# The last feed-forward chunk's way out, spread over the first head of the second attention

## The reference

```
# feed-forward (D_HID = 512)
h = silu(x @ w1.T * w1_s) * (x @ w2.T * w2_s)
h = gelu(h @ h1.T * h1_s)
h = gelu(h @ h2.T * h2_s)
y = h @ w3.T * w3_s                        # 512 -> 128: "the way out"

# differential attention, 8 heads, two components of 8 per head
L1, L2 = cosine scores of component 1 and 2, scaled per head
G  = tanh(delta_gain * (L1 - L2))
A1 = softmax(L1 + G);  A2 = softmax(L2 - G)
y  = (A1 - lambda * A2) @ v,  an RMS norm per head, then @ Wo.T + bo
```

## Time and profile before

| | us |
|---|---|
| median of 3 runs | 706.14 |
| lowest, highest | 706.1, 706.49 |
| the profiled execution | 707.33 |
| its span | 705.5 |
| PE busy | 635.1 (90%) |
| DVE busy | 534.8 (76%) |
| ACT busy | 481.2 (68%) |
| POOL busy | 184.4 (26%) |

### The profile page before, as it was taken

How to read it: one execution, slowest core, us unless ns; L and a number is a source line. 1 busy time by engine, 2 the same in 40 slices (tenths; PEclk the granted TensorE clock), 3 DMA queues, 4 the chain that set the end, 5 groups by cost and what they waited for, 6 DMA issues and landing times.

```text
span 705.5 us, 9380 instructions
## 1 busy us (share of the span) xinstructions
PE 635.1 (90%) x3320; PEld 271.9 (39%) x3320; DVE 534.8 (76%) x1011; ACT 481.2 (68%) x479; POOL 184.4 (26%) x238
## 2 busy tenths in 40 slices
PE   8988899999999989889988888898898788899996
PEld 4666445464464523223222211122231111266555
DVE  6988421517246289999999999999999999676775
ACT  3545324234334399999999999999999989544431
POOL 3431060212102031491147200805600006022012
PEclk9999999999999999999999999999999989999999
DMA  6700200001304402234022510121011204300171
GB/s 193 234 21 1 91 1 0 1 1 36 99 0 135 113 1 57 57 87 140 21 57 84 163 47 11 57 57 56 23 35 57 57 2 121 119 1 1 38 233 30
DMA packets 33598, 44.74 MB, mean 63 GB/s; under 512 B 5520, under 2 KB 19728, under 8 KB 33168
## 3 DMA queue, kind: packets, MB, share of 16 engines
q1 hardware_dynamic: 33552, 44.15, 21.5%
HBM read 31.47 MB, written 10.55 MB: 60 GB/s over the span
## 4 chain that ended last, share of the span: by engine, by line
PE 40%; DVE 23%; ACT 23%; issue 11%; DMA 1%; POOL 1%; SPq 0%; DVEq 0%; ACTq 0%
ACT w_hh L1045 19%; PE ps L731 8%; PE ps L741 8%; DVE hid L1377 5%; DVE hid L1372 5%; PE ps L766 5%; PE ps L713 4%; PE ps L643 3%; PE ps L624 3%; PE ps L697 2%; PE ps L775 2%; DVE st L1147 2%; ACT probs L1016 2%; DMA x_res<-in_x 1%; DVE mx L1224 1%
## 5 line engine op out<-in xcount | busy, mean ns | idle before, releaser
L1045 ACT ACTIVATE w_hh<-hid 128x2048 f32<-128x2048 f32 x128 | 249.9, 1952 | 8.4 <-DVE hid L1377 7.9
L643 PE MATMUL ps<-w_hh,v_h 128*32 128x512 f32 x1024 | 137.8, 610 | 33.3 <-ACT w_hh L1045 32.0
L1372 DVE TENSOR_TENSOR hid<-ps,probs 128x1024 f32<-128x1024 f32 x86 | 104.7, 1217 | 19.3 <-ACT probs L1016 16.1
L624 PE MATMUL ps<-q_s,k_s 64*128 64x512 bf16 x256 | 99.4, 389 | 14.8 <-DVE hid L1372 14.2
L1377 DVE SCALAR_TENSOR_TENSOR hid<-ps,probs 128x1024 f32<-128x1024 f32 x86 | 104.8, 1219 | 4.4 <-PE ps L624 3.3
L624 PE MATMUL ps<-q_w,k_w 64*128 64x512 bf16 x256 | 99.4, 389 | 0.0
L1016 ACT ACTIVATE probs<-ps 128x1024 f32<-128x1024 f32 x86 | 91.2, 1061 | 2.3 <-PE ps L624 2.3
L624 PE MATMUL ps<-q_g,k_s 128*128 128x512 bf16 x256 | 78.3, 388 | 1.1 <-ACT qkv_a L1016 1.1
L624 PEld LDWEIGHTS ps<-q_w,k_w 64*128 64x128 bf16 x256 | 23.7, 93 | 107.2 <-issue 54.5
L741 PE MATMUL ps<-hid,w_hh 128*128 128x512 f32 x128 | 56.3, 592 | 0.0
L731 PE MATMUL ps<-hid,w_hh 128*128 128x512 f32 x128 | 55.8, 593 | 0.0
(11 more groups left out here) (298 smaller groups left out, 991.2 us busy)
## 6 DMA issues: line engine op xcount, KB each, us to landing
qk_rows<-part SPq DMA_DIRECT2D x48, 128.0 KB, 2.4
w_hh<-w_rows SPq DMA_DIRECT2D x4, 1024.0 KB, 9.6
qk_rows<-part_g SPq DMA_DIRECT2D x24, 128.0 KB, 2.4
q_g<-qk_rows SPq DMA_DIRECT2D x32, 96.0 KB, 2.2
k_s<-qk_rows SPq DMA_DIRECT2D x32, 96.0 KB, 2.2
q_s<-qk_rows SPq DMA_DIRECT2D x32, 96.0 KB, 2.4
k_w<-qk_rows SPq DMA_DIRECT2D x32, 96.0 KB, 2.5
q_w<-qk_rows SPq DMA_DIRECT2D x32, 96.0 KB, 2.4
```

The source lines that it names most:

```text
L624: last = mm(ps[:, base + half, :], k_op[rows, u, keys], q_op[rows, u, half * CHUNK:(half + 1) * CHUNK], start=True, stop=True)
L643: last = mm(ps[VW * g4:VW * g4 + VW, 6, :], v_h[:, u, mt, :], ee[:, mt % 2, g4 * CHUNK:(g4 + 1) * CHUNK], start=(mt == 0), stop=(mt == BT ...
L1045: A(ee[:, mt % 2, :], zz[:, mt % 2, :], ACT.Exp).then_inc(S["e"], 1)
L1372: v.tensor_tensor(zz[:, mt % 2, 0:SEQ], banks[:, 2 * CHUNK:4 * CHUNK], gg[s % 3], ALU.add).then_inc(S["z1"], 1)
```

## The change

The table of turns is moved: those of chunk 2 four steps later (v 0 five), those of chunk 3 two to four steps later (late turn one, sums 1 one). The four tiles of the last feed-forward chunk go into the turn bank, one each in the steps (0,1), (0,3), (0,5), (0,7), behind `c_first` and ahead of `c_values`. `b_evac` moves from (0,1) to (1,0), still between the two sums, `b_stats` from (0,2) to (1,1), and the statistics of chunk 3 (`c_in`) from (2,2) to (2,3). SyncE sends chunk 2 after it has loaded head 5. GpSimd builds v_h of heads 4 and 7 ahead of the splits.

```
-SPECIAL = {(0, 2): ("raw", 0), (0, 5): ("raw", 1), (1, 1): ("v", 0), (1, 3): ("sums", 0), (2, 1): ("scale", 0),
+SPECIAL = {(1, 1): ("raw", 0), (1, 3): ("raw", 1), (1, 6): ("v", 0), (1, 7): ("sums", 0), (2, 5): ("scale", 0),
...
-           (4, 5): ("sums", 1), (5, 3): ("scale", 2), (5, 5): ("scale", 3),
+           (4, 6): ("sums", 1), (5, 5): ("scale", 2), (5, 7): ("scale", 3),
...
-                if n in (5, HEADS):
-                    c = 2 if n == 5 else 3
+                if n in (6, HEADS):
+                    c = 2 if n == 6 else 3
...
                 elif kind == "raw":
                     if i == 0:
-                        pe.wait_ge(S["xt_c"], CHUNKS - 1)
+                        pe.wait_ge(S["yo_b"], CHUNKS)
...
             c_prep_turn(late_c - 1)
-            pe.wait_ge(S["qh_c"], 2)
-            for k4 in range(2):
-                b_out_tile(late_c, k4, ps[:, 6, :])
             c_diff(1, 0, 1)
-            b_out_tile(late_c, 2, ps[:, 6, :])
             c_first(1, 0, 1)
-            b_out_tile(late_c, 3, ps[:, 6, :]).then_inc(S["y_b"], 1)
             c_second(1, 0, 1)
...
                         if n == 0:
-                            pe.wait_ge(S["yo_b"], CHUNKS)
+                            pe.wait_ge(S["qh_c"], 2)
+                    if n == 0 and mt % 2:
+                        if mt == 1:
+                            pe.wait_ge(S["xt_c"], late_c)
+                        last = b_out_tile(late_c, mt // 2, turn)
+                        if mt == BT - 1:
+                            last.then_inc(S["y_b"], 1)
                     c_values(s, n % 2, mt)
...
-                    if at == (0, 1):
-                        b_evac(CHUNKS - 1, ps[:, 6, :])
+                    if at == (1, 0):
+                        b_evac(CHUNKS - 1, turn)
                     z_second(n * BT + mt, mt)
...
-                    if at == (0, 2):
+                    if at == (1, 1):
                         b_stats(CHUNKS - 1)
...
-                    if at == (2, 2):
+                    if at == (2, 3):
...
                 if n == 4:
                     late_c_in()
+                    build_v(n)
                     split(late - 1)
...
                 if n == 7:
+                    build_v(n)
                     split(late)
                     split_gained(late)
...
-                if n < NH:
+                if n < NH and n not in (4, 7):
                     build_v(n)
```

More of the change, by code:

```diff
@@ L66 @@
 NH = BATCH * HEADS
-SPECIAL = {(0, 2): ("raw", 0), (0, 5): ("raw", 1), (1, 1): ("v", 0), (1, 3): ("sums", 0), (2, 1): ("scale", 0),
-           (2, 3): ("scale", 1), (3, 1): ("late turn", 0), (3, 3): ("raw", 2), (3, 5): ("raw", 3), (3, 7): ("v", 1),
-           (4, 5): ("sums", 1), (5, 3): ("scale", 2), (5, 5): ("scale", 3),
+SPECIAL = {(1, 1): ("raw", 0), (1, 3): ("raw", 1), (1, 6): ("v", 0), (1, 7): ("sums", 0), (2, 5): ("scale", 0),
+           (2, 7): ("scale", 1), (3, 2): ("late turn", 0), (3, 7): ("raw", 2), (4, 1): ("raw", 3), (4, 3): ("v", 1),
+           (4, 6): ("sums", 1), (5, 5): ("scale", 2), (5, 7): ("scale", 3),
            (9, 7): ("y", 0), (10, 1): ("wo", 0), (10, 3): ("y", 1), (10, 5): ("wo", 1), (11, 5): ("x", 0),
```

## The result

| | before | after |
|---|---|---|
| median of 4 runs each, same chip | 706.32 us | 710.51 us |
| lowest, highest | 706.1, 707.82 | 710.28, 711.2 |
| the profiled execution | 707.33 | 710.55 |
| its span | 705.5 | 708.7 |

The ratio is 1.0056, interval [1.0044, 1.0069]: slower, as forecast, but by 4.2 us (by 3.2 between the two profiled executions), where the sum had 2.1. 710.51 lies just outside the range 706.2 to 710.2. The difference itself is uncertain: the interval is 3.1 to 4.9 us, and in the larger samples on the chips of the experiments the kernel before has medians of 706.71 to 706.85, 0.4 to 0.5 more than in these four runs.

A forecast was written before the change was run, and what follows sets the result against it. VectorE's extra work was taken to make the long steps of the ScalarE-bound second attention. New stalls of 5.95 less 3.86 gone gave net +2.1 us: 706.14 + 2.1 = 708.2, 8 in 10 within 706.2 to 710.2.

The forecast's parts named there:

- The clock.: PE idling in (1,0) and (1,1) was taken to leave the granted clock at 1.00: cost 0.
- the new stall in (1,0): VectorE waits 1.8 us for the last tile at `b_evac`, delaying the second sum: stall 1.68, bounds 1.3 to 1.8.
- The start: Prologue without the tiles: third tanh at 245.2 instead of 246.07, gain 0.87, bounds 0.7 to 1.0.
- PE at half clock in or behind the new stall: Rival: around (1,0), some 3.5 us at clock 0.50 cost up to 1.7, giving 709.9; chance 0.07.
- head 0, (0,3) to (0,5): VectorE's extras leave these steps, gain 0.23; PE's four tiles in head 0 cost 0.
- (1,1), (1,2), (1,3): Steps with no lead left: `acc_out` stalls 0.17, statistics 0.77, emptying raw 0 0.17; sum 1.11.
- (2,1): Chunk 2 sums: today's 0.86, plus 0.44 for nearer v 0 and 0.60 for `acc_out`; 1.90, bounds 1.3 to 2.0.
- (4,1), (5,0), (5,1): Stalls at raw 2 with a wait for PE, 0.25; at sums 1, 0.84; at `acc_out` with no lead, 0.17.
- The lead and the slack of 0.43: VectorE's second sum runs at most 0.78 ahead of its exponential; each step leaves 0.43 for extras, any shortfall stalls.
- The loads: Rival: loads of head 8, needed in step (7,5), come late; with 3 us beyond the cover, 711; chance 0.05.
- no wait: Rival: at (1,0) the last tile lands before VectorE reaches `b_evac`; net -0.2, 705.9; chance 0.13.
- spreading works: Rival: all extras fit, only the waits for sums, 0.86 and 0.84, stay; -2.2, 704.0; chance 0.06.

The follow-up runs named there:

- e7_late_fill: The kernel before with 13 short matmuls added in head 14, in gaps where PE waits for VectorE; 706.48 us, ratio 0.9994.
- e6_spread: The changed kernel with tiles and `b_evac` earlier in head 0, chunk 2 turns moved less and kept apart, prologue gaps filled; 706.23 us, 0.9988 of the kernel before.

## Why the prediction was wrong, step by step

The direction was right, and the mechanism named as decisive was the one that acted. The size was half, and the step that failed is **"The clock."**: it was put at 0 and measured 1.33. Without it the 710.51 would be 709.2, inside the range, and the kernel with the gaps filled did measure 709.07. The step looked for idle time of PE at one place, the new stall in (1,0), found it like a stretch that had kept its clock, and ended "so I take 0". About (1,0) this was right: from 266 to 274 the granted clock of the profile after is 1.00. But the change makes PE idle in another place too. The tiles that leave the prologue were what kept PE busy there: 2.00 of 2 us in both windows before, 0.81 and 0.75 after. "The start" counted their removal as a pure gain and asked only what is late next, not what clock the rest would run at. The rival "PE at half clock in or behind the new stall" had the right mechanism and price (1.7, measured 1.3), at the wrong place and at 0.07. The cover was in view: the waits of 0.64 and 2.14 in the earlier trace rows and the tile in the earlier trace rows say that, without tiles, PE would stand for some of the 4 us ahead of the first exponential. Two of the signs that the prediction set for itself say the same: the low clock moved, and the steps of head 0 were not all 2.705.

By its other steps, against the kernel with the gaps filled, where the clock is out of it (excess over 2.705):

| step | forecast | measured |
|---|---|---|
| start | -0.87 | -0.82 |
| head 0, (0,3) to (0,5) | 0 new, 0.23 gone | 0.11 gone (8.23 instead of 8.34) |
| (1,0) | 1.68 | 1.83 |
| (1,1), (1,2), (1,3) | 0.17, 0.77, 0.17 | 0.15, 0.73, 0.16 |
| (2,1) | 1.90 | 1.79 |
| (4,1), (5,0), (5,1) | 0.25, 0.84, 0.17 | 0.31, 0.84, 0.16 |
| gone: (1,5), (2,3), (4,1), (4,7) | 0.86, 0.68, 0.38, 0.84 | 0.86, 0.68, 0.33, 0.84 |
| net, to (5,1) | 2.1 | 2.34 |

- (1,0) was 0.15 short, most of it the tile: 1.16 us behind the first scores, not the 1.05 that it took behind a difference product. The kernel before has the longer one too, behind its own first scores:

```profile
244.02 1.16 PE L697 MATMUL ps<-w,hid 128*128 128x128 f32 x8
```

- (2,1): VectorE waits 0.92 for the sums, exactly as in the old place, and `acc_out` adds its 0.60. The third part, put at 0.44 for the nearer v 0, was 0.33: PE's sums began 1.32 ahead of the exponential of (2,0) (292.38, 293.70), in the old place 1.65 ahead of that of (1,4) (278.02, 279.67). VectorE, which emptied v 0 just before, came later by as much, so that its own wait did not grow.
- The lead and the slack of 0.43 held: extras of 0.60 and 1.20 with no lead gave 0.15 and 0.73 where 0.17 and 0.77 were due.
- The stalls of (0,4), (1,5), (2,3), (4,7) are gone as forecast, GpSimd and SyncE cost nothing; head 8's first load went out at 407.8, forecast 406.3.
- The loads, "no wait" and "spreading works" did not occur in this kernel. The last is right of another table: with the last tile in (0,5) and the prologue's gaps filled, the 706.23 show that the way out can be spread at no cost. Its profile is 0.43 ahead of before at (5,1), where the rival's sum had 2.2. The waits for the sums, 0.86 and 0.84, are in both; what the rival left out is 0.8 in (1,2) to (1,5), 0.3 at (4,1) and 0.2 more at (1,7), 1.3 of the missing 1.7.

The total in the profiles: 2.34, plus 1.33 for the clock, less 0.4 for one low stretch fewer in head 14, less 0.1 for a first tanh that starts earlier: 3.2, the difference of the spans. What the medians have beyond that, 1.0, stays open. That the profiled execution of before is one of the longer ones (beside `e7_late_fill`) would make some of it, and so would the small number of runs: the interval of the ratio, 3.1 to 4.9 us, holds 3.2.

## What to carry to other kernels

When matmuls are moved out of a stretch where TensorE otherwise waits, read the granted clock and PE's busy time of that stretch with them taken away; they may be what holds the clock for the chain behind it, and a few matmuls without use can be cheaper than the gap. In a loop where one engine has a fixed slack per step, add up the extras of that engine step by step with the lead they find: that arithmetic gave every stall of the changed kernel behind head 0 to 0.15 us (in the spread table, (1,7) came out 0.27 longer than expected). An evacuation that stands ahead of a sum on the critical engine came too early here one step behind the product that it waits for; two steps behind it, in `e6_spread`, it waited for nothing, and behind the sum it cost 1.13 us less.

## What the runs showed of the hardware

- TensorE's clock fell to 1.2 GHz where PE had been busy 0.81 of 2 us and 0.75 of the next 2, in waits of which the longest was 1.19 us, and stayed low for 6.8 us, the last of them with PE busy 1.69 of 2.
- Kernels with the same prologue met it at about 243.4, 248.7 or 248.4 us (worked out from the 0.85, 0.67 and 0.61 of the windows in which it fell), at nearly the same cost of 1.3 to 1.4 us. A granted clock read in one profile is one draw.
- With four matmuls of 128 columns in the first gap, two of six executions had a mean granted clock of 0.999 and 708.7 to 708.8 us, and four had 0.990 to 0.994 and 709.9 to 711.4 us. Thirteen in all the gaps cost nothing that the profile shows and were worth 1.4 us in the median.
- Four fp32 matmuls over 128x128, a tile, took 1.16 us behind first scores and 1.05 behind a difference product, both in the kernel before.
